# A four-layer graph network: the row maxima of the eight-head layer taken one step later, and the normalization's first inverse root moved from ScalarE to GpSimd

## The reference

```python
# eight-head attention, N = 128 nodes, 16 features a head
e = e1[:, :, :, None] + e2[:, :, None, :]            # e1, e2: projections of Wh by head
e = where(adj == 0, -inf, leaky_relu(e, 0.2))
attn = softmax(e, axis=-1)
h = attn @ Wh
...
x = layernorm(x + layer0(x)); x = layernorm(x + layer1(x))
x = layernorm(x + layer2(x)); x = layernorm(x + layer3(x))
# layernorm: (x - mean) / sqrt(var + 1e-5), over the last axis
```

## Time and profile before

| what | value |
|---|---|
| median of 3 runs | 784.14 us (782.19 to 785.19) |
| profiled execution | 782.31 us |
| its span, first to last instruction | 777.4 us |
| mean granted TensorE clock | 0.964 of full speed |
| busy: PE, DVE, ACT, POOL | 688.4, 624.2, 555.6, 402.4 us |

### The profile page before, as it was taken

The page is one execution under the profiler, slowest core; times in us unless marked ns, Lnnn a source line. Parts: engine busy times, 40 slices in busy tenths (PEclk is TensorE's granted clock), DMA queues, the critical chain, the costliest instruction groups (busy, mean ns, idle before and its releaser), DMA issues.

```text
span 777.4 us, 26039 instructions
## 1 busy us (share of the span) xinstructions
PE 688.4 (89%) x8452; PEld 512.0 (66%) x8484; DVE 624.2 (80%) x1786; ACT 555.6 (71%) x1270; POOL 402.4 (52%) x615
## 2 busy tenths in 40 slices
PE   5888989998999588999939999969999999999992
PEld 4566666666666366776739999846666666666661
DVE  2588888888889779999977888866787877878865
ACT  3466656666666499999749999837877778787871
POOL 5487887878888425445431111114646455554641
PEclk9899999999999899999969999969999999999996
DMA  6342433334232212232222333301222222222211
GB/s 171 83 105 69 101 73 95 89 79 101 68 63 43 28 22 35 34 40 35 28 55 68 82 84 91 76 1 22 56 52 50 61 43 58 47 54 47 56 49 42
DMA packets 34907, 47.75 MB, mean 61 GB/s; under 512 B 4389, under 2 KB 18473, under 8 KB 34857
## 3 DMA queue, kind: packets, MB, share of 16 engines
q0 software_dynamic: 18576, 21.01, 16.6%
q1 hardware_dynamic: 15992, 25.97, 10.9%
q10 hardware_dynamic: 288, 0.13, 0.1%
HBM read 51.32 MB, written 8.39 MB: 77 GB/s over the span
## 4 chain that ended last, share of the span: by engine, by line
PE 65%; DVE 21%; issue 7%; ACT 4%; DVEq 2%; DMA 0%; POOL 0%; ACTq 0%; SPq 0%; POOLq 0%
PE banks L1175 7%; PE banks L692 7%; DVE pp L573 5%; PE banks L1490 5%; PE banks L679 4%; PE banks L1501 4%; PE banks L1474 4%; PE banks L1516 4%; PE banks L1464 4%; PE banks L1469 4%; DVE pp L896 3%; PE banks L1508 3%; PE banks L1183 3%; PE banks L669 3%; PE banks L648 3%
## 5 line engine op out<-in xcount | busy, mean ns | idle before, releaser
L573 DVE SCALAR_TENSOR_TENSOR pp<-banks,floor,adj 128x1024 f32<-128x1024 f32 x128 | 157.7, 1269 | 9.2 <-PE banks L679 4.5
L1258 POOL TENSOR_TENSOR pp<-pp,adj 128x512 f32<-128x512 f32 x64 | 73.3, 1161 | 134.9 <-ACT pp L1299 134.9
L490 ACT COPY rows<-banks 128x640 bf16<-128x640 bf16 x64 | 44.3, 692 | 73.5 <-PE banks L669 73.4
L1299 ACT ACTIVATE pp<-banks,nobound 128x512 f32<-128x512 f32 x128 | 81.4, 695 | 3.4 <-PE banks L1490 1.7
L692 PE MATMUL banks<-pp,yv 128*17 128x128 f32 x2048 | 82.0, 278 | 0.1
L798 POOL TENSOR_TENSOR yres<-oo,x 128x512 f32 (+1 forms) x32 | 40.8, 1275 | 69.1 <-DVE oo L914 69.1
L679 PE MATMUL banks<-rows 32*128 32x128 bf16 x1024 | 51.2, 220 | 18.8 <-DVE pp L573 18.7
L1175 PE MATMUL banks<-w2b,xt 128*128 128x256 f32 x256 | 62.1, 387 | 0.0
L1036 POOL DMA_DIRECT2D adj<-in_adj x32 | 17.0, 531 | 80.2 <-ACT sq L1074 80.2
L825 ACT ACTIVATE x<-yres,nmr,rstd 128x128 f32 (+1 forms) x128 | 55.4, 490 | 0.8 <-DVE nmr L126 0.8
L692 PEld LDWEIGHTS banks<-pp,yv 128*17 128x17 f32 x2048 | 45.4, 97 | 14.3 <-issue 0.6
(11 more groups left out here) (208 smaller groups left out, 1938.6 us busy)
## 6 DMA issues: line engine op xcount, KB each, us to landing
adj<-in_adjt POOLq DMA_DIRECT2D x96, 128.0 KB, 3.0
xt<-in_xt SPq DMA_DIRECT2D x32, 256.0 KB, 3.7
x<-in_x SPq DMA_DIRECT2D x32, 256.0 KB, 3.1
adj<-in_adj POOLq DMA_DIRECT2D x32, 256.0 KB, 3.0
out_ngd<-yres SPq DMA_DIRECT2D x32, 256.0 KB, 2.0
ident<-in_ident ACTq DMA_DIRECT2D x1, 64.0 KB, 2.3
w0t<-in_w0t SPq DMA_DIRECT2D x1, 64.0 KB, 2.1
w0e<-in_w ACTq DMA_DIRECT2D x1, 64.0 KB, 2.6
```

Of the source, the lines that this page charges most:

```text
L490: nc.scalar.copy(rows[:, slot % 2, a, :], R[:, 0:5 * N]).then_inc(s["rw"], 1)
L573: nc.vector.scalar_tensor_tensor(pp[:, g], S[g % 2][:, :].rearrange("p (h n) -> p h n", n=N), floor[:, slot:slot + 1], adj[:, slot, g:g + ...
L1258: nc.gpsimd.tensor_tensor(pp[:, slot % 2, h], pp[:, slot % 2, h], adj[:, slot], ALU.mult).then_inc(s["pm"], 1)
L1299: nc.scalar.activation(pp[:, slot % 2, h], S[h][:, :], ACT.Exp, bias=k["nobound"][:, :], scale=SCALE).then_inc(s["p"], 1)
```

## The change

Two things change.

First, in layer 0 `top_lanes`, `top_row`, `top_all` and `top_column` of a batch are taken in one and the same step. Before, `top_lanes(t+4)` and `top_row(t+4)` closed step `t`, and `top_all` and `top_column` followed in step `t+1`. Now in step `t` it is `top_lanes(t+3)` behind the first `weights`, `top_row(t+3)` behind the first `tiles`, `top_all(t+3)` behind the second `weights` and `top_column(t+3)` behind the second `attend`. ScalarE's `copy_shift(t+3)` and `factors(t+3)` move behind `evac_sums(t, 0)` and `evac_turned(t-1, 1)`.

Second, `roots` is one instruction of GpSimd, a power with exponent -0.5, in place of two of ScalarE. Newton's step stays. The pieces of the difference below are, in order: `roots`; layer 0's GpSimd tail; layer 0's step on ScalarE, VectorE and TensorE; and layer 1's start on GpSimd (layers 2 and 3 have the same line there, layer 3 behind its first two mask loads and without a tail) and on ScalarE. At the end of layers 1 and 2 portion 0 moves to GpSimd in the same way, in layer 1 ahead of the last residual, in layer 2 ahead of layer 3's first mask loads.

```diff
-    def roots(self, act, portion):
+    def roots(self, pool, portion):
...
-        act.wait_ge(self.var, portion + 1)
-        nc.scalar.activation(self.rstd[:, c], self.v[:, c], ACT.Ln).then_inc(self.log, 1)
-        act.wait_ge(self.log, portion + 1)
-        nc.scalar.activation(self.rstd[:, c], self.rstd[:, c], ACT.Exp, scale=-0.5).then_inc(self.root, 1)
+        pool.wait_ge(self.var, portion + 1)
+        nc.gpsimd.tensor_tensor(self.rstd[:, c], self.v[:, c], self.half[:, :].to_broadcast([N, c.stop - c.start]), ALU.pow).then_inc(self.root, 1)
...
@@ -450,6 +448,7 @@
         def tail():
+            after.roots(pool, 0)
             divide(T - 1, (T - 1) % RING)
...
@@ -528,15 +527,15 @@
...
-            if in3:
-                copy_shift(t + 3, a3)
             if in1:
                 bases(t + 1, a1)
-            if in3:
-                factors(t + 3, a3)
             evac_sums(t, 0)
+            if in3:
+                copy_shift(t + 3, a3)
             if not known(t) or t >= 1:
                 evac_turned(t - 1, c0, 1)
+            if in3:
+                factors(t + 3, a3)
...
@@ -598,24 +596,23 @@
...
             if not known(t) or t + 3 < T:
-                top_all(t + 3, a3)
+                top_lanes(t + 3, a3)
             if not known(t) or t >= 1:
                 weights(t, 1, slot, lap)
+            if not known(t) or t + 3 < T:
+                top_all(t + 3, a3)
             weights(t, 2, slot, lap)
...
-            if not known(t) or t + 4 < T:
-                top_lanes(t + 4, slot)
...
@@ -732,9 +728,11 @@
...
             if in3:
-                top_column(t + 3, a3)
+                top_row(t + 3, a3)
             scores(t, 3, slot)
             attend(t, 1, slot)
+            if in3:
+                top_column(t + 3, a3)
...
-            if in4:
-                top_row(t + 4, slot)
...
@@ -803,6 +799,7 @@
...
         layer0.tail()
+        before.roots(pool, 1)
...
@@ -852,7 +853,6 @@
...
         row_exp(0, 0)
-        before.roots(act, 1)
         evac_xt(1, 1)
```

More of the change, by code:

```diff
@@ L82, with __init__ @@
 class Rows:
-    def __init__(self, nc, sb, sem, L, stats, cut):
-        self.nc, self.stats, self.cut = nc, stats, cut
+    def __init__(self, nc, sb, sem, L, stats, half, cut):
+        self.nc, self.stats, self.half, self.cut = nc, stats, half, cut
         self.mean, self.rstd, self.nmr, self.d, self.v = (sb(f"{n}{L}", [N, B], F32) for n in ("mean", "rstd", "nmr", "dev", "var"))
-        self.link, self.var, self.log, self.root, self.done = (sem(f"rows{L}_{n}") for n in ("link", "var", "log", "root", "done"))
+        self.link, self.var, self.root, self.done = (sem(f"rows{L}_{n}") for n in ("link", "var", "root", "done"))
     def columns(self, portion):
@@ L530, in step @@
                 evac_rows(t + 1, 0, a1)
+            if in1:
+                bases(t + 1, a1)
+            evac_sums(t, 0)
             if in3:
                 copy_shift(t + 3, a3)
-            if in1:
-                bases(t + 1, a1)
+            if not known(t) or t >= 1:
+                evac_turned(t - 1, c0, 1)
             if in3:
                 factors(t + 3, a3)
-            evac_sums(t, 0)
-            if not known(t) or t >= 1:
-                evac_turned(t - 1, c0, 1)
             if in4:
@@ L551, in _ @@
         evac_turned(T - 1, (T - 1) % RING, 0)
-        after.roots(act, 0)
         evac_turned(T - 1, (T - 1) % RING, 1)
@@ L600, in _ @@
         top_all(2, 2, c_zero)
-        top_lanes(3, 3)
         def step(t, slot, lap):
@@ L722, in _ @@
         pe.wait_ge(s["sh"], 3)
-        top_row(3, 3)
         def step(t, slot, lap):
@@ L813, in _, with tail @@
         steps(pool, step, end, R8)
-        block.tail = lambda: residual(T - 1, (T - 1) % R8)
+        def tail():
+            after.roots(pool, 0)
+            residual(T - 1, (T - 1) % R8)
+        block.tail = tail
     @block.scalar
@@ L1924, in layers @@
     const = constants(nc, sb, sem, pb, c, k)
-    r0, r1, r2 = (Rows(nc, sb, sem, L, stats, (T - 2) * NG) for L in range(3))
+    r0, r1, r2 = (Rows(nc, sb, sem, L, stats, k["minushalf"], (T - 2) * NG) for L in range(3))
     l0 = multi(nc, place0, sem, pb, k, yres, stats, rall, const, r0, c["x"], c["xt"], c["adjt"])
```

## The result

| | before | after |
|---|---|---|
| median | 783.29 us (782.19 to 785.19, 6 runs) | 832.5 us (827.79 to 834.8, 6 runs) |
| profiled execution | 782.31 us | 833.12 us |
| its span | 777.4 us | 827.9 us |
| mean granted TensorE clock | 0.964 | 0.923 |
| busy: PE, DVE, ACT, POOL | 688.4, 624.2, 555.6, 402.4 us | 695.9, 622.2, 561.0, 463.9 us |

The changed kernel is slower: ratio 1.0621, 95% interval 1.0589 to 1.0653. The prediction was 778.7 us, range 768 to 789. It was to be faster by 0.7% and is slower by 6.2%: the direction and the size are both wrong.

A forecast was written before the change was run, and what follows sets the result against it. Layer 0 was taken as bound by a ring through TensorE, ScalarE's copy and VectorE's maximum, neither engine full. 782.31 - 11.6 (layer 0) + 6.2 (power) = 776.9, plus 1.8 to the median: 778.7 us, range 768 to 789.

The forecast's parts named there:

- P: Time of GpSimd's power of 120 columns at the three layer ends, taken as 3.0 us, bounds 0.40 and 5.6.
- the slow rival: Layer ends: power takes many microseconds, uncovered, each us costing three; at 8 us the kernel takes 793.7; chance 0.20.
- 3P - 2.81: Sum over the three layer ends of what GpSimd's power adds to the kernel: 6.2 us.
- P - 0.47: End of layer 0: Newton's step starts later by this; less 0.35 for ScalarE's two small activations, 2.18 us.
- P - 0.65: End of layer 1: power, then last residual on GpSimd stretching Newton's first product; 2.35 us added.
- P - 1.34: End of layer 2: Newton's step, before held by other VectorE work, now follows the power; 1.66 us added.
- the wait for the shift: Layer 0: TensorE's next projection waits for ScalarE's copy of the shift, taken as 0.3 us a step.
- TensorE's own step: Layer 0: TensorE's work per step without waits, 6.64 us plus about 0.15 for the row's product: 6.79.
- VectorE's new ring: Layer 0: VectorE's weights and maximum with TensorE's row product, at most 6.82 us a step, no bound above TensorE's.
- pay for being first: Rival, end of layer 0: first power costs once extra, 780 with 1.28 us, 784.7 with about 6; chance 0.06.
- The cheap power: Rival, layer ends: power takes up to 1 us, ends change by under 1 us, kernel about 772; chance 0.15.
- TensorE doesn't wait for the shift: Rival, layer 0: no wait, 6.79 us a step, saving 19.7 us, 770.6 with the power; chance 0.10.

The follow-up runs named there:

- e5_small_power: e3_shift_first with the 8-column portion's root moved to GpSimd's power, the 120 columns staying on ScalarE: 761.92 us, ratio 0.9711.
- e3_shift_first: e1_order_only with ScalarE's copy of the shift put ahead of the copy of the sums: 761.91 us, ratio 0.9719.
- e1_order_only: Changed kernel with the roots back on ScalarE, so only layer 0's new order remains: 777.28 us, ratio 0.9905.
- e6_shift_old_place: e3_shift_first with the shift's copy back at its place before the change, ahead of the bases' exponentials: 767.47 us, ratio 0.9781.
- e8_shift_first_again: Kernel of e3_shift_first unedited, run again on one chip with e9_old_place_again: 763.03 us, ratio 0.9743.
- e2_power_only: Kernel before the change with only the roots moved to GpSimd's power, layer 0's order as before: 838.9 us, ratio 1.0701.
- e7_half_power: Order of before; GpSimd's power takes 60 of the 120 columns and the 8, ScalarE the other 60: 809.88 us, ratio 1.0325.
- e4_power_price: e3_shift_first plus ten unused GpSimd instructions (powers and a product) behind its last step: power of 120 columns 19.46 us, product 0.39.
- e9_old_place_again: Kernel of e6_shift_old_place unedited, run again on one chip with e8_shift_first_again: 762.33 us, ratio 0.9724.

## Why the prediction was wrong

**The step that failed is the power's price.** The prediction took "P = 3.0, because it is not simple arithmetic and GpSimd has no faster row than VectorE", between bounds of 0.40 and 5.6. It measured 19.54, 19.87 and 19.49. The rows it stood on were of other functions and another engine: VectorE's reciprocal and GpSimd's products. They gave 23.6 ns an element, the power needs 160. The upper bound was no bound: "both functions twice as long" was a factor of choice. The direction of the whole forecast hung on P, since from 6.1 us on the kernel is over 0.5% slower, and the slow rival, which had the mechanism and the threefold price right, got 0.20 and a worked case of 8 us.

**The structure of the power term held.** With 3P - 2.81 and the measured mean of 19.63 the term is 56.1; its parts:

- End of layer 0, P - 0.47: Newton's start moved by 11.23 while the variance came 7.80 earlier, 19.03 with P = 19.54, so P - 0.51.
- End of layer 1, P - 0.65: from the variance to the end of Newton's first product there were 2.38 us and are 21.64 (431.37 - 409.73), 19.26 more, with P = 19.87. The last residual stands behind the power (429.96) and the product beside it takes 1.36 us, where it takes 0.28 alone. The rule of the Trainium skill (Advanced Engine Details and Errata, GPSIMD Details), that the two engines conflict where VectorE reads two operands in SBUF, was drawn on for this; by it, the trace agrees.
- End of layer 2, P - 1.34: 19.90 from variance to Newton, 1.71 before: 18.19 with P = 19.49.
- The 0.35 us of the small activations is seen in e5_small_power, and the small powers, 1.65 to 1.70 instead of 0.4, stay hidden.

**Layer 0: the mechanism was right, the wait for the shift too small.** TensorE's own step of 6.79 us was exact (e3_shift_first). VectorE's new ring was no bound. The wait's cost was taken as 0.3 a step and is 0.48: 7.27 a step instead of 7.09. (The row of the projection shows 0.24, the part in which TensorE had nothing else to do.) After the second attention products (end 112.29) come 0.14 to the copy of the sums, 0.48 to the shift's, 0.17 for it and 0.14 back, 0.93 in all, where 0.75 was put together; the two hand-overs had been taken as 0.06. Against 0.53 without a wait that is 0.40; the next scores then follow 0.67 behind the projection and not 0.59, since the weight load waits too. Over 27 steps the saving is 6.8 us where 11.6 was forecast; the whole of layer 0 shows 7.8. The other 1.0 is 1.9 gained ahead of the steps (a projection at 33.23 that stood at 35.15) and 0.9 lost behind them (8.7 ahead at the last step's projection, 222.11 for 230.77, and 7.8 at the variance). At the start TensorE's clock was up sooner, with a granted mean of 0.96 from 20 to 60 us and of 0.91 before. Some of that may be this execution's luck: e1_order_only has the same step, a granted clock of 0.87 there, and its layer 0 ends only 6.0 earlier than before.

**What the prediction didn't have: how long TensorE stays at the lower clock level.** In both profiles TensorE starts layer 1 at the lower of its two levels (1.2 GHz; its first products take 1.12 us before and 1.11 after, at a granted clock of 0.50). In the changed kernel it keeps it for longer. Its products in the kernel before, and behind them the same after:

```profile
270.38 1.55 PE L974 MATMUL banks<-xt,wa1rep 128*128 128x512 f32 x2
271.77 0.60 PE L962 MATMUL banks<-ident,x 128*128 128x128 f32 x4
```

```profile
281.61 1.92 PE L973 MATMUL banks<-xt,wa1rep 128*128 128x512 f32 x2
...
283.32 1.06 PE L961 MATMUL banks<-ident,x 128*128 128x128 f32 x4
```

Layer 1 was to shrink by 0.35 and grew by 1.1, layer 2 grew by 0.7: together 2.2 us. It is tempting to blame the stop, which grew from 4.3 to 22.9 us, but the other profiles speak against it. e6_shift_old_place has the roots on ScalarE and a stop of 4.29 us, and takes as long for the same products, as e1_order_only and e8_shift_first_again do:

```profile
252.26 1.91 PE L975 MATMUL banks<-xt,wa1rep 128*128 128x512 f32 x2
253.97 1.06 PE L963 MATMUL banks<-ident,x 128*128 128x128 f32 x4
```

From Newton's first product to the variance of layer 1 there are 135.04, 135.07 and 135.03 us in the three kernels with a large power (the changed one, e2_power_only, e7_half_power), and 133.7 to 136.9 in the eight profiles with these roots on ScalarE; the kernel before, at 133.92, is one of the shortest. Layer 2, from the end of Newton's first product to its variance, takes 106.69 in the changed kernel, 105.9 to 106.1 in those eight, and 105.37 in e2_power_only, which has the same stops. So the 2.2 us are no price of the power that the runs could show; in layer 1 they are within what profiles without it differ by, and in layer 2 the cause stays open. At the start of layer 3 the lot fell the other way: from 10 to 20 us behind Newton's start the granted clock is 1.00 in e2_power_only and 0.83 in the changed kernel, with the same power ahead of both, and layer 3 takes 267.5 and 269.9 us.

**The sum again, with measured sizes:** 782.31 - 7.8 + 56.1 + 2.2 = 832.8, and the profiled execution took 833.12. All four terms are read from the same two traces, so the sum only closes the account and tests nothing. The tests are e1_order_only and e2_power_only, which add up, and e7_half_power.

**The other rivals.** The first power doesn't pay for being first: 19.54 against 19.87 and 19.49. It also began 0.17 us after the variance was ready (254.95). The 6 us that the Trainium skill (GPSIMD Engine Reference, Instruction dispatch) puts on the first call of freshly loaded code don't show here. The cheap power is refuted by e4_power_price. "TensorE doesn't wait for the shift" isn't so in this kernel, and its 6.79 a step is what the kernel gets once the copy stands first: e3_shift_first and e8_shift_first_again, at 0.972 and 0.974 of the time before, are better than both kernels, with e9_old_place_again their equal (0.972).

## What to carry to other kernels

An operation that no row of the trace shows has no upper bound from rows of other operations: where the sign of a forecast hangs on its price, and it stands three times where nothing else can run, the chance must be split by where the price turns the sign, not gathered around a guess. Here the root of 120 columns belongs on ScalarE, in two activations of 0.30 us each; GpSimd's power did no harm with 8 columns that nobody waits for, and gave no gain that the runs could tell. When a small copy shares an engine with large ones and a full engine waits for it, try it ahead of them: one line moved gave twice what the rest of the reordering had gained (15.4 us after 6.9).

## What the runs showed of the hardware

- GpSimd's power: 0.30 us and 0.160 us for each element of a partition's row, from 32 to 120 of them; the same with exponents of -0.5 and 2, variances or a constant as base, and 16 or 128 partitions (e4_power_price). The product of the same shape takes 0.39 us for 120 elements.
- One kernel's executions differ with the moment at which TensorE's clock reaches its upper level: by 3.8 and 4.5 us at the start of the kernel and by 2 us at the start of layer 1. The medians of one and the same kernel in two jobs were 767.47 and 762.33 us. On this kernel 5 us between two jobs are no evidence; two kernels are to be compared in one job, with a look at these rows in both profiles.
- The length of the stop ahead of a layer doesn't settle how its first products run: two of layer 1's groups took 1.92 and 1.06 us behind a stop of 22.9 us, 1.91 and 1.06 behind one of 4.29 (e6_shift_old_place), and 1.55 and 0.60 behind one of 4.29 in the kernel before.
